# Causal mask of layer A's last four batches added by TensorE, ranks over the blocks summed by TensorE, and changed orders at the layer ends

## The reference

```python
x = x + attn_a(_layernorm(x), ...)     # 16 heads of 8, causal
x = x + ffn(_layernorm(x), ...)
x = x + attn_b(_layernorm(x), ...)     # 16 heads, no mask, per-head scale and shift of the scores
x = x + ffn(_layernorm(x), ...)
...
scores = jnp.einsum('bhqd,bhkd->bhqk', q, k) * scale
mask = jnp.triu(jnp.full((t, t), NEG, jnp.float32), k=1)
attn = jax.nn.softmax(scores + mask, axis=-1)
...
logits = flat_x @ Wr                                  # 8 experts
top_vals, top_idx = jax.lax.top_k(logits, 2)
g = ...Wg; u = ...Wu; h = jax.nn.silu(g) * u          # hidden 512
out = sum over the two chosen experts of weight * (h @ Wd) * DEPTH_SCALE
```

## Time and profile before

| | us |
|---|---|
| median of 3 runs | 1205.51 (1203.42 to 1205.73) |
| profiled execution | 1201.22 |
| its span | 1198.8 |
| busy: PE, DVE, ACT, POOL | 1031.9, 763.5, 672.4, 538.9 |

### The profile page before, as it was taken

One profiled execution on the slowest core, in us unless ns is written; L12 is line 12 of the kernel. 1 busy time (PEld: TensorE's weight loads), 2 busy tenths in 40 slices (PEclk: granted clock), 3 DMA queues, 4 the chain that ended last, 5 costly groups with the idle time before them and its releaser, 6 DMA issues.

```text
span 1198.8 us, 28758 instructions
## 1 busy us (share of the span) xinstructions
PE 1031.9 (86%) x9198; PEld 719.2 (60%) x9198; DVE 763.5 (64%) x2364; ACT 672.4 (56%) x1399; POOL 538.9 (45%) x1010
## 2 busy tenths in 40 slices
PE   3998999896789989999798879998977689899990
PEld 1444555452358889999444434443443489899990
DVE  5687777968548333366778888888767573234442
ACT  2465767553524445555377769887836445455550
POOL 2243444333850630344688645655626416103555
PEclk9999999996858999999778889998967799999995
DMA  6355444662125877887644324333121258778974
GB/s 158 92 133 142 100 103 98 179 140 61 40 70 154 267 230 235 258 270 221 143 110 100 97 56 108 82 92 84 44 56 58 91 171 282 217 227 263 280 218 111
DMA packets 201722, 175.02 MB, mean 146 GB/s; under 512 B 19812, under 2 KB 160616, under 8 KB 201576
## 3 DMA queue, kind: packets, MB, share of 16 engines
q1 hardware_dynamic: 193384, 156.41, 47.4%
q0 software_dynamic: 8192, 16.79, 4.7%
HBM read 122.99 MB, written 50.14 MB: 144 GB/s over the span
## 4 chain that ended last, share of the span: by engine, by line
PE 44%; DVE 15%; POOL 9%; issue 6%; DMA 4%; SPq 1%; ACT 1%; POOLq 0%; ACTq 0%; DVEq 0%
PE psS L1358 9%; PE psT L1365 9%; PE psO L316 4%; PE psN L1381 4%; PE psO L1381 4%; PE psS L350 3%; POOL xn L1259 3%; DVE mx L662 3%; POOL prow L736 2%; PE psO L959 2%; PE psN L323 1%; PE psT L358 1%; PE psM L1346 1%; DMA eo<-ysb 1%; POOL part L749 1%
## 5 line engine op out<-in xcount | busy, mean ns | idle before, releaser
L662 DVE TENSOR_REDUCE mx<-psS 128x3 f32<-128x384 f32 (+1 forms) x512 | 311.1, 617 | 117.9 <-PE psS L377 62.4
L350 PE MATMUL psS<-kst,qst 48*128 48x256 bf16 (+1 forms) x1024 | 200.9, 284 | 57.2 <-DVE mx L662 42.6
L549 ACT ACTIVATE pT<-psT,scb 128x512 f32<-128x512 f32 x256 | 194.0, 778 | 56.7 <-PE psT L358 55.3
L1421 DVE TENSOR_TENSOR hT<-sg,psT 128x512 f32<-128x512 f32 x142 | 97.5, 686 | 160.3 <-PE psT L1365 126.1
L358 PE MATMUL psT<-qst,kst 50*128 50x256 bf16 (+1 forms) x1024 | 194.0, 279 | 5.4 <-DMA qst<-scr_m 2.4
L1245 POOL DMA_INDIRECT xg<-xn,slot x128 | 123.5, 965 | 149.9 <-DVE ysb L1416 86.5
L780 POOL TENSOR_SCALAR_AFFINE_SELECT pT<-pT 128x256 f32<-128x256 f32 x256 | 104.0, 414 | 134.0 <-ACT pT L544 132.2
L350 PEld LDWEIGHTS psS<-kst,qst 48*128 48x128 bf16 x1024 | 65.7, 97 | 156.8 <-DVE mx L662 82.7
L1358 PE MATMUL psS<-xTt,wgc 128*128 128x128 f32 x1136 | 153.5, 279 | 5.0 <-issue 5.0
L544 ACT ACTIVATE pT<-psT 128x384 f32<-128x384 f32 x256 | 122.6, 491 | 57.7 <-PE psT L358 56.2
L1365 PE MATMUL psT<-xTt,wuc 128*128 128x128 f32 x1136 | 151.8, 277 | 0.4 <-DMA wuc<-in_L_ffn_Wu 0.3
(11 more groups left out here) (227 smaller groups left out, 1605.2 us busy)
## 6 DMA issues: line engine op xcount, KB each, us to landing
wgc<-in_L_ffn_Wg SPq DMA_DIRECT2D x142, 256.0 KB
wuc<-in_L_ffn_Wu SPq DMA_DIRECT2D x142, 256.0 KB
scr_part<-part SPq DMA_DIRECT2D x128, 128.0 KB, 2.1
qst<-scr_part SPq DMA_DIRECT2D x64, 192.0 KB, 3.7
kst<-scr_part SPq DMA_DIRECT2D x64, 192.0 KB, 4.5
xin<-xg SPq DMA_DIRECT2D x142, 64.0 KB
eo<-ysb SPq DMA_DIRECT2D x142, 64.0 KB
scr_part<-part SPq DMA_DIRECT2D x32, 192.0 KB, 1.9
```

The source lines that it names most:

```text
L350: return nc.tensor.matmul(ps[:, c0:c0 + n], q_[r64, t, q0], k_[r64, t, 0:n], start=(half == 0), stop=True, skip_group_check=True)
L549: nc.scalar.activation(pT[:, g % 8, 0:cols], psT[g % 2][:, 0:cols], ACT.Exp, scale=scb[r][:, 0, i:i + 1], bias=scb[r][:, 1, i:i + 1]).then ...
L662: nc.vector.tensor_reduce(mx3[:, u, 0:n, pos:pos + 1].rearrange("p a b -> p (a b)"), psS[h % 2][:, 0:kcols(L)].rearrange("p (a k) -> p a k ...
L1421: nc.vector.tensor_tensor(out=hT[(n0 + k) % FETCH][:].rearrange("p a c -> p (a c)"), in0=sg[p][:], in1=psT[p][:], op=ALU.mult).then_inc(f[ ...
```

## The change

1. For layer A's batches 12 to 15 (MASKED = 12) TensorE adds a mask `tritb` to the two diagonal blocks of `psT` with one more matmul per head, ahead of the exponential; GpSimd's L780 is left out for them and `pv_quad` waits for the exponential alone.
2. `pe_counts` sums over the blocks too: 16 matmuls with ones, each over the blocks behind block k, accumulate onto the triangle's ranks and give the totals. Part 3 of the route and two operations of part 6 go.
3. Parts move: in both attention layers the parts 8 and 2 of the first half stand at step 18, h = 15; in the FFN the parts stand a tile earlier, and so do the gates of the scatters.
4. The layer-norm statistics and tokens of blocks 16 to 27 in step 18 are spread over the heads.
5. In layer B the 16 `xn` operations of GpSimd stand eight behind the split of step 14 and eight behind that of step 15.
6. The dummy Silu, which loads ScalarE's table, moves from the end of step 19 to behind the first two tiles' copies.
7. `tritb` is made at the start (two more operations on GpSimd).

```diff
             def pv_quad(b, r, q):
-                after(pe, s["pT"], 16 * b + 4 * q + 4)
+                if L.causal and b >= MASKED:
+                    after(pe, s["exp"], 16 * b + 4 * q + 4)
+                else:
+                    after(pe, s["pT"], 16 * b + 4 * q + 4)
...
                 if T_:
                     last_t = scores_t(1)
+                    if L.causal and bT >= MASKED:
+                        diag = psT[1 - par][:, 0:3 * P].rearrange("p (a k) -> p a k", a=3)[:, 0:3:2, :]
+                        last_t = nc.tensor.matmul(diag, identb[:], tritb[:].unsqueeze(1).to_broadcast([P, 2, P]),
+                                                  start=False, stop=True, skip_group_check=True)
...
             nc.tensor.matmul(count_bank(n)[:, 0:w], triu[:], rhs, start=True, stop=True, skip_group_check=True)
-            nc.tensor.matmul(count_bank(n)[:, w:2 * w], onesb[:], rhs, start=True, stop=True,
-                             skip_group_check=True).then_inc(r["cnt_ps"], 1)
+            for k in range(size):
+                upper = size + 2 if k < PART else size + 1
+                last = nc.tensor.matmul(bank[:, k + 1:upper, :], onesb[:],
+                                        pickb[:, k:k + 1, :].to_broadcast([P, upper - k - 1, E]),
+                                        start=False, stop=True, skip_group_check=True)
+            last.then_inc(r["cnt_ps"], 1)
...
-                link(nc.vector.tensor_tensor(out=b, in0=a, in1=cnt, op=ALU.subtract))
-                link(nc.vector.tensor_tensor(out=a, in0=b, in1=pre, op=ALU.add))
...
-                    pool.wait_ge(f_sem["y"], n0 + ROUTE_SLOT + pair // 2)
+                    pool.wait_ge(f_sem["y"], n0 + ROUTE_SLOT - 1 + pair // 2)
                 else:
-                    pool.wait_ge(f_sem["u"], n0 + ROUTE_SLOT + 3 + pair // 2)
+                    pool.wait_ge(f_sem["u"], n0 + ROUTE_SLOT + 2 + pair // 2)
...
             if k == 0:
                 tokens(0)
                 tokens(1)
+                nc.scalar.activation(junk[0:1, 0, 0:1], ones_row[0:1, 0:1], ACT.Silu)
...
-                if l == 1 and j == 15 and h == 1:
+                if l == 1 and j in (14, 15) and h == H:
                     pool.wait_ge(s_ln[2], 1)
-                    for k in range(SIZE[0]):
+                    for k in range((j - 14) * SIZE[0] // 2, (j - 13) * SIZE[0] // 2):
...
-                if l == 0 and j == 16 and h < 6:
-                    dve_route_part(dve, 0, h + 3)
+                if l == 0 and j == 16 and h < 4:
+                    dve_route_part(dve, 0, h + 4)
...
+                if l == 1 and j == 16 and 12 <= h < 16:
+                    dve_route_part(dve, n, h - 8)
+                if j == 18 and h == 15:
+                    dve_route_part(dve, n, 8)
+                    dve_route_part(dve, n, 2)
+                if j == 18:
+                    if h == 0:
+                        dve.wait_ge(x1, NBLK - 4)
+                    dve_ln_at(dve, h, SIZE[0], NBLK - 4 - SIZE[0], s_ln[n + 1], 1)
+                    if 10 <= h < 14:
+                        dve_tokens(dve, n + 1, SIZE[0] + 3 * (h - 10), SIZE[0] + 3 * (h - 9))
```

More of the change, by code:

```diff
@@ L40 @@
 PCH = 23
+MASKED = B - 4
 POS = [8 * (h // 8) + 4 * (h % 2) + (h % 8) // 2 for h in range(H)]
@@ L98, in build @@
         trib = sb("trib", [P, P], BF16)
+        tritb = sb("tritb", [P, P], BF16)
         ones_row = sb("ones_row", [1, T])
@@ L146, in build @@
         pickb = sb("pickb", [P, SIZE[0], E], BF16)
-        counts = sb("counts", [P, 2, SIZE[0], E])
+        counts = sb("counts", [P, max(SIZE) + 2, E])
         v12 = sb("v12", [P, 3, SIZE[0]])
@@ L358, in scores_t @@
                     return nc.tensor.matmul(ps[:, c0:c0 + T - q0], k_[m64, t, half * P:half * P + P], q_[m64, t, q0:T],
-                                            start=True, stop=True, skip_group_check=True)
+                                            start=(half == 0 or not L.causal), stop=True, skip_group_check=True)
                 if S_:
@@ L1024, in dve_counts @@
             size = SIZE[n % G]
-            nc.vector.tensor_copy(counts[:, :, 0:size, :],
-                                  count_bank(n)[:, 0:2 * size * E].rearrange("p (a k e) -> p a k e", a=2, e=E)).then_inc(r["cnt"], 1)
+            nc.vector.tensor_copy(counts[:, 0:size + 2, :].rearrange("p k e -> p (k e)"),
+                                  count_bank(n)[:, 0:(size + 2) * E]).then_inc(r["cnt"], 1)
             dve.wait_ge(r["cnt"], n + 1)
@@ L1119, in dve_route_part @@
                 link(nc.vector.tensor_tensor(out=w[:, 1, :], in0=w[:, 0, :], in1=e_, op=ALU.mult))
[L1120 to L1133, removed]
+            rank, total, part = counts[:, 0:size, :], counts[:, size, :], counts[:, size + 1, :]
+            a, b, further = ea_, eb_, lg[:, 0:size, :]
             down, up = upto[:, 0, 0, :], upto[:, 0, 1, :]
@@ L1147, in dve_route_part @@
             if stage == 4 and g == 1:
-                link(nc.vector.tensor_tensor(out=upto[:, 0], in0=a[:, PART - 1:2 * PART:PART, :],
-                                             in1=lim[1][:].unsqueeze(1).to_broadcast([P, 2, E]), op=ALU.subtract))
+                nc.vector.tensor_tensor(out=down, in0=part, in1=lim[1][:], op=ALU.subtract)
+                link(nc.vector.tensor_tensor(out=up, in0=total, in1=lim[1][:], op=ALU.subtract))
                 link(nc.vector.tensor_scalar(upto[:, 0], upto[:, 0], 0.0, float(P - 1), ALU.max, ALU.add))
@@ L1183, in dve_route_part @@
             if stage == 6:
-                link(nc.vector.tensor_tensor(out=b, in0=a, in1=cnt, op=ALU.subtract))
-                link(nc.vector.tensor_tensor(out=a, in0=b, in1=pre, op=ALU.add))
-                link(nc.vector.tensor_tensor(out=b, in0=a, in1=each(lim[g][:]), op=ALU.is_ge))
+                link(nc.vector.tensor_tensor(out=b, in0=rank, in1=each(lim[g][:]), op=ALU.is_ge))
                 link(nc.vector.tensor_tensor(out=b, in0=b, in1=each(step_up[:]), op=ALU.mult))
                 if g == 1:
-                    link(nc.vector.tensor_tensor(out=further, in0=a, in1=each(lim[2][:]), op=ALU.is_ge))
+                    link(nc.vector.tensor_tensor(out=further, in0=rank, in1=each(lim[2][:]), op=ALU.is_ge))
                     link(nc.vector.tensor_tensor(out=further, in0=further, in1=each(step_b[:]), op=ALU.mult))
                     link(nc.vector.tensor_tensor(out=b, in0=b, in1=further, op=ALU.add))
-                link(nc.vector.tensor_tensor(out=a, in0=a, in1=each(below[g][:]), op=ALU.add))
+                link(nc.vector.tensor_tensor(out=a, in0=rank, in1=each(below[g][:]), op=ALU.add))
                 link(nc.vector.tensor_tensor(out=b, in0=a, in1=b, op=ALU.add))
@@ L1626, in hook @@
                     act_tokens(act, 2 * l + 1, h // 2)
-                if j == 19 and h == 15:
-                    nc.scalar.activation(junk[0:1, 0, 0:1], ones_row[0:1, 0:1], ACT.Silu)
                 if l == 0 and j == 19 and h == 14:
@@ L1755, in _ @@
             nc.gpsimd.memset(trib[:], 0.0).then_inc(s_const, 1)
-            pool.wait_ge(s_const, 2)
+            nc.gpsimd.memset(tritb[:], 0.0).then_inc(s_const, 1)
+            pool.wait_ge(s_const, 3)
             nc.gpsimd.affine_select(out=ident[:], in_=ident[:], compare_op=ALU.not_equal, fill=1.0, base=0,
@@ L1760, in _ @@
                                     pattern=[[-1, P]], channel_multiplier=1).then_inc(s_const, 1)
+            nc.gpsimd.affine_select(out=tritb[:], in_=tritb[:], compare_op=ALU.is_ge, fill=NEG, base=0,
+                                    pattern=[[1, P]], channel_multiplier=-1).then_inc(s_const, 1)
             for r in range(RING):
@@ L1790, in _ @@
             dve.wait_ge(s_lnA, 1)
-            dve.wait_ge(s_const, 4)
+            dve.wait_ge(s_const, 6)
             nc.vector.tensor_copy(identb[:], ident[:]).then_inc(s_const_dve, 1)
@@ L1805, in _ @@
         def _(pe):
-            pe.wait_ge(s_const, 4)
+            pe.wait_ge(s_const, 6)
             pe_setup(pe, LA)
```

29 lines of the change are left out of this document (9 added, 20 removed).

## The result

| | before | after |
|---|---|---|
| median, us | 1205.62 (1203.42 to 1211.88, 4 runs) | 1165.02 (1162.78 to 1168.44, 4 runs) |
| ratio | | 0.9658 (95%: 0.9612 to 0.9703) |
| profiled execution, span | 1201.22, 1198.8 | 1162.78, 1161.0 |
| mean granted clock | 0.906 | 0.927 |

A forecast was written before the change was run, and what follows sets the result against it. TensorE bounds layer A's steady steps; VectorE and GpSimd are short at layer ends. Layer A's end -11.3, FFN 1 -2.9, layer B -12.1, FFN 2 -3.4 sum to -29.7 us: 1176 us, range 1164 to 1189.

The forecast's parts named there:

- the clock comes back fully: Rival: TensorE busy enough in every stretch but the last, 9 us more there, -40 in all, 1165 us; chance 0.13.
- Layer A, 301 to 362: Layer A's end: GpSimd waits -7.6, masks +4.2, spread statistics -1.2, clock -6; sum -10.6 us.
- 6 of the 15: Layer A, 301 to 362: a full clock would give back up to 15 us; 6 were taken.
- What is late next is the exponential on ScalarE: Layer A's step from 322.8 to 346.4: ScalarE, 10.2 us busy, keeps it from falling below some 14 us.
- +2.0 in 246 to 273: Layer A, where TensorE bounds: 16 added masks at a pitch of 0.12 us cost +2.0 us.
- The slower rival: Rival: each added matmul stands for its whole record and the clock gain fails, +6.6, 1212 us; chance 0.03.
- Route of the first half, layer A: Layer A, 273 to 301: VectorE loses 6.4 us, counts +2.2, masks +1.9; net -2.3 us.
- signs of being wrong: Layer A's end: clock row still 0.5 to 0.6, or normalise(0) of step 19 now waiting for part 8.
- +2.2 us: Layer A's route: TensorE's 16 count matmuls at 0.14 us each, with VectorE waiting for them.
- Layer B: Layer B: tokens -3.4, route -3.9, statistics -4.4, Silu -0.4; together -12.1 us.
- The gains overlap: Rival: half of layer B's 12 us and a part of FFN's go, -22, 1183 us; chance 0.15.
- FFN: Both FFNs: heads -0.2 each, earlier scatters -2.7 and -3.2; FFN 1 -2.9, FFN 2 -3.4 us.

The follow-up runs named there:

- run 1: The kernel before with only the masks of batches 12 to 15 on TensorE (parts 1 and 7 of the change): 1197.41 us, ratio 0.9917.
- run 3: The changed kernel with the statistics and tokens of blocks 16 to 27 in one block again in step 18, both layers: 1176.51 us, ratio 0.9760.
- four corners: Kernels with neither edit, statistics spread, masks on TensorE, both; from step 16's marker to the first gate 60.7, 58.8, 51.6, 44.3 us.
- run 9: The changed kernel with the first transposed score matmul of each head issued three times in the two route stretches: 1170.81 us, ratio 0.9707.
- run 10: The changed kernel with each new mask of batches 12 to 15 issued twice, at half the value: 1169.19 us, ratio 0.9707.
- run 11: The changed kernel with TensorE's mask for the last three batches only, GpSimd zeroing batch 12 as before: 1160.95 us, ratio 0.9646.
- run 8: The changed kernel with parts 8 and 2 of the first half back in the route, both layers: 1171.12 us, ratio 0.9713.
- run 4: The changed kernel with the sums over the blocks back on VectorE, orders and gates as changed: 1171.63 us, ratio 0.9697.
- run 5: The changed kernel with GpSimd's 16 token operations of layer B in one block ahead of step 15's split: 1172.27 us, ratio 0.9711.
- run 12: The changed kernel with the gates of the second half's scatters one more tile earlier: 1159.58 us, ratio 0.9617.
- run 7: The changed kernel with the Silu that loads ScalarE's table back at the end of step 19: 1164.86 us, ratio 0.9657.

## Why the prediction was right, and where it was off

The direction and the places were right, the size was not: 29.7 us were summed and 38.4 came. The time equals the rival's "the clock comes back fully", for two reasons of which that is one. The range took it in by 1 us only.

**Layer A, 301 to 362: the term that was mis-sized.** I took -7.6 for the waits for GpSimd, -1.2 for the spread statistics, "less than in B since GpSimd was late there too", and "6 of the 15" for the clock. TensorE's idle time fell by 9.0 us (12.7 to 3.7), which is the first two together, 8.8. But run 1 and run 3 show how it is shared out: the masks alone take away 4.6, since a wait of 4.8 us for the residual stands at once where GpSimd's stood, and the spreading takes the rest. "What is late next is the exponential on ScalarE" was wrong: next was VectorE's block, and behind that TensorE itself, at 15.8 of 16.2 us. From step 17's marker to the last quad 25.7 us became 16.2; the step that I had put at 16 to 18 instead of 23.6 so takes some 14, the floor that I had named, though another engine sets it.

**The clock** was the rest. TensorE was busy 48.1 us at a clock of 0.67, 15.9 us above the full clock's; it is now busy 40.6 at 0.93, 2.8 above. By that product 13 of the 16 came back. The busy time itself says a little less: it fell by 7.5 us although 34 masks were added, 4.1 us at 0.12, so the clock gave 11.6. With that the terms add up: 9.0 of idle time, plus 11.6, less 4.1 for the masks, are 16.5 us, and 16.4 were measured. Either way it was about twice the 6 that I took, and this is the term that was mis-sized. The clock rose as the idle time fell: 0.67, 0.70, 0.84, 0.93 for 12.7, 12.2, 7.8, 3.7 us in the four corners above; that the idle time is the cause is argued, since the masks also gave TensorE more to do. Only the last chain keeps a low clock (0.76), as I expected of it. I had allowed for the chain and underrated the step before it. The rule of the Trainium skill that I had weighed ("TensorE: Matmul & The Clock Gate", "A second HAM failure mode: psum-queue depth-cycling", short idles between groups of matmuls make the clock go to and fro) would have left this stretch low. Steps 17 and 18 at 1.00 do not test it, as the idle time itself went (0.06 and 0.36 us are left); the trace agrees in layer B's route, 0.65 with TensorE busy 90% of the time. That the idles there hold the clock down was not shown: in run 9 layer A's route had 0.9 us of idle time instead of 3.0, at the same clock of 0.78, and in layer B's the added matmuls did not fill it.

**Masks.** The pitch of 0.12 us is what the timeline of step 17 shows between the new mask (L382) and the next matmul; by the length of the step a second mask cost 0.087 (run 10). The +2.0 in 246 to 273 was about right in size: the stretch grew by 1.0 us in run 1, and is 1.6 to 2.5 longer in the changed kernels than in run 11, which has GpSimd's mask there. But it does not go by the number of masks: 14 more in run 10 left it at 29.3 us, at a clock of 0.93 instead of 0.88, so a part of the growth is the clock's. The slower rival, by which each must stand for its whole record, is refuted: by the time of 1165 us, by run 10 for a mask behind a mask, and for the change from score matmuls to a mask by the timeline of step 17. There the new mask starts 0.15 us behind the last score matmul, as the old mask did in the kernel before, and the old mask now 0.12 us behind the new one.

**Route of the first half, layer A.** -2.3 forecast, -5.2 in the profile, -3.5 to -5.2 by the kernels with the same code. Parts 8 and 2 had about the right price: 3.85 forecast, 3.2 to 4.9 and 2.9 by run 8, and 1 us comes back at the last step, as I had warned ("up to 2 us"). That is also one of the signs of being wrong that I had named: in layer A normalise(0) of step 19 stands directly behind the moved parts, without idle time of VectorE ahead of it. It cost 1 us; the forecast had put it at nothing. The term that was off is "+2.2 us" for the counts: 16 of them take 1.1 us at a clock between the two levels (from 279.47 to the next score matmul at 280.58):

```profile
279.36 0.31 PE L980 MATMUL psM<-pickb,triu 128*128 128x128 bf16 x1
279.47 1.18 PE L983 MATMUL psM<-pickb,onesb 128*128 128x136 bf16 x16
280.58 0.28 PE L355 MATMUL psS<-kst,qst 48*128 48x128 bf16 x1
```

The slots came 8.6 us after the counts instead of 13.5, 4.9 earlier, not 3 to 4. By run 4 the sums on TensorE are worth 2.3 us or more here, with the clock in it, and at most 0.65 in layer B.

**Layer B.** -12.1 forecast, -14.3 in the profile. Route -3.9 (made with 6.1 us of VectorE, where layer A's parts sum to 6.4) against -4.6; statistics -4.4 against 3.8 by run 3. The tokens were priced too low, -3.4 against 6 by run 5: I had counted TensorE's wait of 2.7 us and 0.7 behind it, but what stood on the path was VectorE's wait for GpSimd's chain ahead of the seed, 5.4 us. "The gains overlap" is thereby ruled out: in runs 3, 5 and 8 parts of layer B's change were undone singly and each gave back 3.8, 6 and 2 us.

**FFN.** A forecast of -6.3, -6.7 in the profile, but that agreement is in part luck. Run 1, which has the FFN of the kernel before, took 238.1 and 206.2 us in the two, against 236.9 and 208.9 before; the eight kernels with the changed FFN took 236.1 and 205.5 on the mean. That is some 1.5 and 2 us, about half of what was forecast, with a spread as large. Seen at the tiles, the lateness at tile 24 fell, but 1.3 and 1.8 us of it stayed, not 0.8; in run 12 it is gone at tile 24 of both, so it was still the scatters. The heads gave little: up to tile 12 the gates of FFN 2 that are late by over 0.25 us sum to 5.7 us instead of 7.1. The Silu gave nothing (run 7) where I had 0.4 twice.

**What stays open.** The start took 1.9 us longer in the profile after; the same code took from 227.6 to 229.4 us to step 13 in the others but for one (235.6), so I put no cause to it. The last 2.2 us of the 40.6 are those by which the profiled executions lie apart from the medians.

## What to carry to other kernels

- When a wait is removed, look for what stands behind it in the same step: another engine may be late for the same matmul. From step 16 to the gate the masks alone gave 9.3 us here and their undoing cost 14.5, since two engines were late in the same step: price such edits as a pair, and give the interaction to neither.
- Where an engine waits at the end of a chain that crosses three, price the first wait of the chain (VectorE's 5.4 us for GpSimd), not the last that you see (TensorE's 2.7).
- A stretch at a low clock can hold a second gain behind the first, here some 12 us beside 9 us of waits. In the corners above 12 us of idle time in 59 went with 0.70, 8 in 52 with 0.84, 4 in 44 with 0.93.
- Before a stretch's difference is put down to an edit, look how far it varies in kernels with the same code: 5 us in FFN 1 here, 0.02 in step 17.

## What the runs showed that I had not expected

- A bf16 mask matmul of 2x128 columns behind others starts 0.12 us after the one ahead and lengthened a TensorE-bound step by 0.087 us (run 10), and 16 matmuls with ones of up to 136 columns take 0.7 us in the FFN head at the full clock, some 0.03 us from one to the next; their records last 0.22 to 0.28.
- More matmuls did not raise the clock: in layer B's route 22 added ones left it at 0.61 (0.65 without) and lengthened the stretch by 4.9 us, 0.22 each.
- Layer B's route has no engine that is full at what it does, TensorE 19.5 and VectorE 16.8 of 21.65 us, and yet it took 21.55 to 21.76 us in eight of the nine kernels with the same code there (22.9 in run 10), while the clock in it read from 0.64 to 0.74. So in this range the clock does not set its length; what does stays open.
